# Four-layer convolution chain: the filter loads of the lag convolution move from SyncE's queue to ScalarE's

## The reference

```python
x = x + _L0_conv_ref(_gn(x), ...)   # rational filter, 16 x 16 channel pairs
x = x + _L1_conv_ref(_gn(x), ...)   # patch mixer with 8 x 8 patches
x = x + _L2_conv_ref(_gn(x), ...)   # 3 x 3 convolution
x = x + _L3_conv_ref(_gn(x), ...)   # rational filter again, other weights

# layers 0 and 3
h = irfft2(rfft2(b, s=(128, 128)) / rfft2(a, s=(128, 128)))
Y = einsum('...hwi,ijhw->...hwj', rfft2(x, s=(256, 256)), h0 + rfft2(h, s=(256, 256)))
y = irfft2(Y)[..., :128, :128, :]
```

## Time and profile before

| | us |
|---|---|
| median of 3 runs | 3450.89 |
| lowest and highest | 3450.52, 3458.02 |
| the profiled execution | 3437.14 |
| its span | 3435.4 |
| TensorE busy | 3238.6 (94% of the span) |
| ScalarE busy | 1685.3 (49%) |
| VectorE busy | 1568.5 (46%) |
| GpSimd busy | 1253.5 (36%) |

### The profile page before, as it was taken

One profiled execution on the slowest core, in us unless ns is written; L12 is line 12 of the kernel. 1 busy time (PEld: TensorE's weight loads), 2 busy tenths in 40 slices (PEclk: granted clock), 3 DMA queues, 4 the chain that ended last, 5 costly groups with the idle time before them and its releaser, 6 DMA issues. The chain is left out here.

```text
span 3435.4 us, 82654 instructions
## 1 busy us (share of the span) xinstructions
PE 3238.6 (94%) x37276; PEld 2667.3 (78%) x37276; DVE 1568.5 (46%) x1939; ACT 1685.3 (49%) x1766; POOL 1253.5 (36%) x1018
## 2 busy tenths in 40 slices
PE   6999999899999899999899999999989987799998
PEld 6999998589998666666687776666678773499998
DVE  6787887411112444435755533333665444411112
ACT  3666665555563444444554534444454430455552
POOL 5888887165562012222620001222370000155551
PEclk9999999999999999999999999999999998999999
DMA  0333334877778312122233322121221345877776
GB/s 21 106 124 118 118 124 149 262 205 197 199 203 203 103 57 90 66 82 74 74 117 92 105 104 98 50 98 50 77 95 56 93 133 80 195 203 200 199 198 173
DMA packets 261513, 428.67 MB, mean 125 GB/s; under 512 B 28391, under 2 KB 110441, under 8 KB 259689
## 3 DMA queue, kind: packets, MB, share of 16 engines
q1 hardware_dynamic: 245178, 396.67, 39.9%
q10 hardware_dynamic: 15984, 26.72, 2.3%
HBM read 305.88 MB, written 113.77 MB: 122 GB/s over the span
## 5 line engine op out<-in xcount | busy, mean ns | idle before, releaser
L138 PE MATMUL m_bank<-p_xn,p_w 128*128 128x512 f32 x1536 | 618.9, 403 | 33.0 <-PEq L18 11.8
L139 PE MATMUL m_bank<-p_xn,p_w 128*128 128x512 f32 x1536 | 603.3, 393 | 0.0
L140 PE MATMUL m_bank<-p_xn,p_w 128*128 128x512 f32 x1536 | 602.8, 392 | 0.0
L827 PE MATMUL c_acc<-c_shifted,filt 128*32 128x240 f32 (+8 forms) x11264 | 457.5, 317 | 13.5 <-issue 13.5
L827 PEld LDWEIGHTS c_acc<-c_shifted,filt 128*32 128x32 f32 x11264 | 442.4, 159 | 24.7 <-issue 22.7
L605 ACT ACTIVATE filt<-filt 64x2048 f32<-64x2048 f32 (+3 forms) x256 | 426.3, 1767 | 14.9 <-DMA filt<-filters_dram 11.2
L129 ACT ACTIVATE p_w<-p_raw_weights 128x2048 fp32r<-128x2048 f32 x96 | 373.2, 3888 | 122.2 <-PE m_bank L140 100.6
L592 POOL TENSOR_TENSOR filt<-filt 64x1408 f32<-64x1408 f32 x64 | 259.5, 4055 | 473.1 <-DMA filt<-filters_dram 473.1
L138 PEld LDWEIGHTS m_bank<-p_xn,p_w 128*128 128x128 f32 x1536 | 291.3, 190 | 174.1 <-issue 78.6
L133 DVE TENSOR_TENSOR p_w<-p_raw_weights,p_w 128x2048 fp32r<-128x2048 f32 x86 | 333.3, 3875 | 159.8 <-ACT p_w L129 159.8
L140 PEld LDWEIGHTS m_bank<-p_xn,p_w 128*128 128x128 f32 x1536 | 291.3, 190 | 62.9
(11 more groups left out here) (200 smaller groups left out, 6590.4 us busy)
## 6 DMA issues: line engine op xcount, KB each, us to landing
c_shifted<-spectrum_dram SPq DMA_DIRECT2D x256, 270.0 KB, 3.9
filters_dram<-stage SPq DMA_DIRECT2D x124, 512.0 KB, 3.5
filt<-filters_dram SPq DMA_DIRECT2D x248, 256.0 KB, 4.8
p_raw_weights<-in_L_conv_Wq SPq DMA_DIRECT2D x16, 2048.0 KB, 8.7
p_raw_weights<-in_L_conv_Wk SPq DMA_DIRECT2D x16, 2048.0 KB, 8.5
p_raw_weights<-in_L_conv_Wv SPq DMA_DIRECT2D x16, 2048.0 KB, 8.6
m_qf<-in_L_conv_Wout SPq DMA_DIRECT2D x128, 256.0 KB, 3.8
spectrum_dram<-c_shifted SPq DMA_DIRECT2D x116, 136.0 KB, 2.5
```

Of the source, the lines that this page charges most:

```text
L138: pe.matmul(out, w[0], x[0], start=first, stop=False)
L139: pe.matmul(out, w[0], x[1], start=False, stop=False)
L140: return pe.matmul(out, w[1], x[0], start=False, stop=last)
L827: mm = nc.tensor.matmul(acc[k % 2][phase][32 * s:32 * s + 32, 0:B, LAGS * kb:HALF], filt[:, k, phase, :, :, 4 * kb + s].rearrange("p j c - ...
```

## The change

In the steady part of the loop (groups 4 to 31) SyncE issues only the four row loads, at points 0, 2, 4 and 6 of the running group. The filter loads of group g + 3 go to ScalarE's queue: two quarters ahead of `move_odd` of group g and two behind it, each pair after a wait for the end of group g - 1. The opening loop on SyncE is written out for groups 2 and 3 without `piece`; what it issues, and at which points, stays as it was.

```diff
@@ -613,7 +613,7 @@
     RUN = B * ROW - LAGS
     FAR_AT, FAR = 2 * LAGS * NEAR, L - 2 * LAGS * NEAR
     POINTS, HALVES_DONE = 11, 6
-    SPREAD = (0, 1, 2, 3, 5, 6, 7, 8)
+    SPREAD = (0, 2, 4, 6)
     LAST_PAIR, FETCH_AT = 7, 5
     LAST_BATCH = RING * (N_BATCHES - 1)
     QUARTERS = 4
@@ -713,12 +713,6 @@
             f = FW * c + 4 * (g - GROUPS // 2) + s
             eng.dma_start(prod[f:f + 1, 1], out[32 * s + c:32 * s + 32:2, g % RING].rearrange("p b t q -> p (b t q)")).then_inc(last_in, 16)
 
-        def piece(eng, g, k, m):
-            if m < 4:
-                load_filters(eng, filt, scratch, layer, g, k, m).then_inc(filt_in[k], 16)
-            else:
-                load_rows(eng, g, k, m - 4)
-
         @block.sync
         def _(sp):
             if staged is not None:
@@ -745,20 +739,22 @@
             for k in range(4):
                 sp.wait_ge(rows_stored[k], 32 * (2 * C // 4))
 
-            for m in range(8):
+            for m in range(4):
                 if m:
                     sp.wait_ge(progress, m)
-                piece(sp, 2, 2, m)
-                if m >= 4:
-                    piece(sp, 3, 3, m - 4)
-            for m in range(4, 8):
+                load_filters(sp, filt, scratch, layer, 2, 2, m).then_inc(filt_in[2], 16)
+            for m in range(4):
                 sp.wait_ge(progress, 4 + m)
-                piece(sp, 3, 3, m)
+                load_rows(sp, 2, 2, m)
+                load_filters(sp, filt, scratch, layer, 3, 3, m).then_inc(filt_in[3], 16)
+            for m in range(4):
+                sp.wait_ge(progress, 8 + m)
+                load_rows(sp, 3, 3, m)
             for n in range(1, N_BATCHES):
                 for k in range(RING):
-                    for m in range(8):
+                    for m in range(4):
                         sp.wait_ge(progress, POINTS * (RING * (n - 1) + k + 1) + SPREAD[m])
-                        piece(sp, RING * n + k, k, m)
+                        load_rows(sp, RING * n + k, k, m)
 
             def load_products(m):
                 par, pair, c = m // C, m % C // 2, m % 2
@@ -1114,9 +1110,18 @@
                 act.dma_start(scratch["products"][4 * (RING * n + k):4 * (RING * n + k) + 4].rearrange("s j c n -> (s j c) n"),
                               out[:, k].rearrange("p b t q -> p (b t q)")).then_inc(prod_stored[k], 16)
 
+            def fetch(g, quarters):
+                act.wait_ge(progress, POINTS * (g - RING + 1))
+                for q in quarters:
+                    load_filters(act, filt, scratch, layer, g, g % RING, q).then_inc(filt_in[g % RING], 16)
+
             lower_half(1)
             for g in range(GROUPS):
+                if RING <= g + RING - 1 < GROUPS and g:
+                    fetch(g + RING - 1, range(0, 2))
                 move_odd(*divmod(g, RING))
+                if RING <= g + RING - 1 < GROUPS and g:
+                    fetch(g + RING - 1, range(2, 4))
                 if g + 2 < GROUPS:
                     lower_half(g + 2)
                 if g < GROUPS - 1:
```

## The result

The changed kernel takes 3530.69 us (median of 3 runs, 3513.38 to 3535.53) against 3450.89: the ratio is 1.0196, interval 1.0153 to 1.0239. (A ratio in this document is not the quotient of two medians, which would be 1.0231 here.) It was forecast to be 2.5 us faster and is 80 us slower. Measured again in a later set of runs, beside the kernel before, its ratio was 1.0207 (1.0169 to 1.0244). Its profiled execution has a span of 3528.9 us, 93.5 us more than that of before.

A forecast was written before the change was run, and what follows sets the result against it. TensorE was taken as the bound, idle only for late instruction packets. All terms were 0 except the entry's -2.5 us: 3450.89 - 2.5, rounded to 3448 us, range 3435 to 3461.

The forecast's parts named there:

- What bounds the kernel: Both loops: TensorE busy 94% of the span; its 31.0 us idle is instruction packets late because DMA engines are full.
- SyncE: Its queue loses 224 filter issues, 135 us of queue time, none on the path: credit 0.
- ScalarE: Its queue gains 112 issues per convolution; copies move by 1.2 us at most, with 10 us of slack: cost 0.
- The filters' arrival: Last quarter of a group's filters lands at about T + 13.4, T being the group's start; 6 us left: cost 0.
- The row loads: Four row loads per group move to points 0, 2, 4, 6 and only get earlier: credit 0.
- The DMA stream: Steady loop: same bytes, two bursts possible per group, no net difference for instruction packets: 0, bounds 22.7 us either way.
- the two entry stalls: TensorE's stalls of 3.93 and 4.4 us at the loops' entries, near 698 and 3002 us, forecast to stay.
- The entry: Start of each loop: fewer transfers behind groups 2 and 3 shrink later gaps of 4.4 us in sum: -2.5 us.
- The bursts: Rival, slower: instruction packets wait behind three transfers in each group's two bursts; 12.5 us, giving 3463 us; chance 0.19.

The follow-up runs named there:

- the small filters: Changed kernel with the filter loads of groups 4 to 31 cut to 8 numbers per piece: 3409.2 us, ratio 0.9866, loops 758.1 us.
- One queue: Kernel before with the changed timing of filters and rows, all on SyncE's queue: 3512.7 us, ratio 1.0171, loops 866.6 us.

## Why the prediction was wrong

- *What bounds the kernel.* Right: TensorE's idle time is "issue", before and after, and it is late instruction packets, as the prediction inferred: every gap over 0.5 us ends 1.2 to 1.8 us after such a packet, and the small filters show that DMA traffic causes it.
- *SyncE.* Right, 0: none of its waits reached TensorE.
- *ScalarE.* Right in size. L1109 (now L1105) still waits for TensorE; the copies started 1.1 us late in the group shown and in the mean of the first loop, 2.1 us at most (forecast at most 1.2), and no wait of TensorE names them.
- *The filters' arrival.* Right: 5.8 us to landing, 1 us more, with no effect.
- *The row loads.* "They only get earlier. Credit: 0." This looked at who reads them and not at what they stand beside. With pairs, and kept away from them (0, 4, 9, 10), rows gave loops of 802.2; at 0, 2, 4, 6 they gave 868.6 to 883.5.
- *The DMA stream.* This step failed: "I see no net difference for an instruction packet in the steady loop and take 0; the bounds are the loss of all gaps but the two entry stalls, 31.0 - 3.93 - 4.4 = 22.7 us, and as much again". It counted work by the mean rate, 275 GB/s, alike for every transfer. The runs show that transfers are not alike: the loss is there with filters into half of the partitions close to rows, and gone with the same bytes into all of them (792.2 and 787.4). The term was 0 and measured +89 us: 63 us more in gaps and 25 us in matmuls that ran longer, most of that by the lower granted clock around the gaps, for which the sum had no term. The upper bound was also no bound: it took the gaps that were there for the most that a new arrangement could add, though nothing in the rows limits a late packet to that.
- *The entry.* -2.5 us did not come. TensorE's longest wait in the first entry fell from 3.9 to 3.3 us, but its waits from 680 to 720 us rose from 6.9 to 8.8 us in sum, and the DMA share there rose from 0.93 to 0.98; set against 89 us it does not matter.
- *The rivals.* The bursts (which the prediction also calls the third rival) had the right sign (chance 0.19) and half of the place: of the 54 gaps over 0.5 us, 25 begin 8 to 11 us into a group, but only the two entry stalls at 3 to 5. Their price was 12.5 us, a seventh of the measured one, and the reason was wrong: bursts on two queues. One queue makes 72 of the 89 us, and a burst of four rows makes nothing. By what the prediction worked out from the Trainium skill's rule on queue rows served in turn, two queues with work should have been slower than one; spaced transfers on two queues were not (0.9977).

What is shown: the loss is in the two loops; TensorE's gaps end with the arrival of instruction packets; the loss needs the narrow filter loads (two kernels, 91 and 79 us less with wide ones) and the row loads; it comes with timing and for the most part not with the queue; spacing the transfers undoes it. What is argued: that narrow writes hold up the DMA engines in front of the instruction packets; the mean packet times above do not settle it. The Trainium skill's "DMA: Bandwidth & Descriptors", section "Back-pressure in remote DMA", has for transfers between cores that stalled writes also stall the other queues of the same DMA engine; something like it may be at work in the local transfers here, but no run shows that step. Open: why one meeting of a pair with rows costs nearly as much as two, and what the 24 to 31 us without a pair come from.

## What to carry to other kernels

Before moving a DMA in time, ask what else is in flight there and how many partitions it writes; its own reader's slack is only half of the question. Where the profile calls TensorE's idle time "issue" and DMA engines are busy, treat the instruction stream as one more user of them, and keep narrow transfers (into few partitions) apart from others in time. Look at the granted clock around gaps as well: part of the cost can lie in matmuls that run longer. A bound on what can be lost must not be taken from what is lost now.

## What the runs showed of the hardware that was not expected

- With the same 256 KB per load written to 64 instead of 128 partitions, ScalarE's queue (filters and stores) took 119 instead of 97 ns per packet, and the other queue's packets 125 instead of 97 ns.
- Cutting 1.02 MB of narrow filter loads per group gave loops of 758.1 us, cutting 1.08 MB of row loads 793.8 us: the narrow bytes cost 36 us more (device times 3409.2 and 3442.1 us).
- A DMA issue on ScalarE's queue ran beside an ACTIVATE (945.16 beside 945.15), but the next ACTIVATE waited for the pair to be issued.
- Idle time of TensorE that reads "issue" ended 1.2 to 1.8 us after the end of an instruction packet (q8), in all 75 gaps over 0.5 us in the loops of both kernels.
- Gaps of 1 to 4 us came with a lower granted clock: 0.50 from 803 to 806 us behind a gap of 3.20 us, 0.98 over the loops with 93.8 us of gaps, 1.00 over those with 31.0.
